# Attention beside a scan: decays in the halves of the context's place in SBUF, turned states in two banks of PSUM

## The reference, cut to what matters

```
x = x + tanh(g_xattn) * ssm(ctx, layernorm(x))
    # state_t = state_{t-1} * exp(delta_t * A[:, n]) + delta_t * u_t * B_t[n]
    # y_t     = sum_n state_t[:, n] * C_t[n]            n = 0..15
x = x + tanh(g_ffn) * layer(layernorm(x))
    # layer: RMS norm, causal attention, output product, RMS norm,
    #        8 routed experts (best 2 per row) and a shared expert
```

## Time and profile before

| What | us |
|---|---|
| median of 3 runs (1787.08 to 1792.86) | 1789.75 |
| the profiled execution | 1790.59 |
| its span, first to last instruction | 1788.8 |
| units of round 0 (attention 0 beside scan 1), 234.6 to 397.2 | 162.6 |
| units of round 1, 481.7 to 645.0 | 163.3 |
| units of round 2, 727.0 to 892.0 | 165.0 |
| DVE busy in the units of round 0 | 149.6 |
| POOL busy in the units of round 0 | 95.9 |

### The profile page before, as it was taken

How to read it: one execution, slowest core, us unless ns; L and a number is a source line. 1 busy time by engine, 2 the same in 40 slices (tenths; PEclk the granted TensorE clock), 3 DMA queues, 4 the chain that set the end, 5 groups by cost and what they waited for, 6 DMA issues and landing times.

```text
span 1788.8 us, 26797 instructions
## 1 busy us (share of the span) xinstructions
PE 1503.7 (84%) x9168; PEld 1150.6 (64%) x9168; DVE 1166.9 (65%) x1699; ACT 916.2 (51%) x2038; POOL 810.2 (45%) x807
## 2 busy tenths in 40 slices
PE   5677967788777789677878998799999999999994
PEld 2344645565445556455655666688787999999973
DVE  5987589996699985899945444432324666566545
ACT  5675457764467753567724663221213666666510
POOL 1992266542466532565413211243422555555444
PEclk8789968899878899788988999899999999999997
DMA  4460001111011111011132004721311877777464
GB/s 168 153 229 19 25 23 55 54 43 54 7 35 55 54 36 31 19 47 54 37 123 95 30 32 160 293 77 59 110 37 65 307 243 253 261 241 253 155 221 165
DMA packets 94664, 195.76 MB, mean 109 GB/s; under 512 B 8945, under 2 KB 25841, under 8 KB 91201
## 3 DMA queue, kind: packets, MB, share of 16 engines
q1 hardware_dynamic: 89408, 177.26, 29.1%
q0 software_dynamic: 5120, 16.78, 2.8%
HBM read 140.40 MB, written 53.61 MB: 108 GB/s over the span
## 4 chain that ended last, share of the span: by engine, by line
PE 55%; DVE 16%; issue 15%; POOL 7%; ACT 5%; DMA 1%; SPq 1%; DVEq 0%; ACTq 0%; POOLq 0%
PE scores L631 21%; PE bank L631 14%; DVE HS L1770 6%; DVE YA L1781 4%; PE bank L705 3%; PE bank L775 3%; POOL GB L2281 2%; PE bank L790 2%; ACT bank L1269 2%; PE bank L825 2%; PE scores L762 2%; POOL yab L2471 2%; PE scores L749 1%; PE bank L1092 1%; PE scores L765 1%
## 5 line engine op out<-in xcount | busy, mean ns | idle before, releaser
L2281 POOL TENSOR_TENSOR GB<-DU,BB 128x512 f32<-128x512 f32 x256 | 326.8, 1298 | 36.1 <-DVE DL L1752 21.2
L1770 DVE TENSOR_TENSOR_SCAN HS<-bank,GB 128x512 f32<-128x512 f32 x224 | 272.0, 1214 | 20.3 <-ACT bank L1269 17.6
L705 PE MATMUL bank<-ident,HS 128*128 128x128 f32 x860 | 165.8, 325 | 120.9 <-DVE YA L1781 104.9
L705 PEld LDWEIGHTS bank<-ident,HS 128*128 128x128 f32 x860 | 115.2, 165 | 166.3 <-DVE YA L1781 129.8
L1269 ACT ACTIVATE bank<-DL,aneg 128x512 f32<-128x512 f32 x224 | 154.7, 691 | 110.0 <-DVE HS L1770 108.2
L775 PE MATMUL bank<-ident,EX 128*128 128x128 f32 x640 | 131.5, 306 | 34.2 <-ACT PT L1314 20.9
L631 PE MATMUL scores<-xth,wgh 128*128 128x256 f32 x552 | 158.1, 286 | 2.2 <-DVE fa L2162 1.3
L1781 DVE SCALAR_TENSOR_TENSOR YA<-bank,Ct,YA 128x512 f32<-128x512 f32 x199 | 147.0, 738 | 14.2 <-PE bank L705 12.8
L631 PE MATMUL scores<-xth,wgl 128*128 128x256 f32 x552 | 156.1, 283 | 0.0
L631 PE MATMUL scores<-xtl,wgh 128*128 128x256 f32 x552 | 156.1, 283 | 0.0
L1314 ACT ACTIVATE PT<-bank 128x128 f32<-128x128 f32 (+3 forms) x256 | 110.3, 431 | 72.0 <-PE bank L775 64.9
(11 more groups left out here) (294 smaller groups left out, 3798.6 us busy)
## 6 DMA issues: line engine op xcount, KB each, us to landing
wgr<-wffn_in SPq DMA_DIRECT2D x108, 384.0 KB, 6.5
wdr<-wffn_in SPq DMA_DIRECT2D x81, 256.0 KB, 3.1
BB<-b_scratch SPq DMA_DIRECT2D x64, 256.0 KB, 3.3
xr<-xg SPq DMA_DIRECT2D x23, 512.0 KB, 5.8
yg<-ysb SPq DMA_DIRECT2D x23, 512.0 KB, 6.5
xg<-V SPq DMA_DIRECT2D x11, 1024.0 KB, 5.8
hah<-hhd SPq DMA_DIRECT2D x5, 1024.0 KB, 14.1
hal<-hhd SPq DMA_DIRECT2D x5, 1024.0 KB, 16.1
```

The source lines that it names most:

```text
L705: mm = nc.tensor.transpose(state_bank(s, q)[:, et * P:(et + 1) * P], HS[:, n % 2, et, tt * P:(tt + 1) * P], ident[:])
L1770: nc.vector.tensor_tensor_scan(HS[:, n % 2, et, :], decay_bank(s, k), GB[:, k % 4, :], 0.0, ALU.mult, ALU.add).then_inc(scan_done, 1)
L2281: nc.gpsimd.tensor_tensor(GB[:, k % 4, :], DU[:, et, :], BB[:, n % 2, :], ALU.mult).then_inc(gb_ready, 1)
```

## The change

Decays of the scans beside attention go by turns into the two halves of `cT` in SBUF instead of the bank HT1, and decay k waits for scan k - 2. HT1 becomes a second bank of turned states: states go by turns into HT0 and HT1, and turn q waits for the addition of state q - 2. The next context can't be loaded into `cT` while decays use it, so its load moves from the start of the round to its end and waits for all 64 blocks of the scan. Nothing else changes.

```diff
             if s == 0:
                 return (HT0, A[0])[q % 2]
-            return (A[0], A[2], A[3])[q - (NB - 3)] if q >= NB - 3 else HT0
+            return (A[0], A[2], A[3])[q - (NB - 3)] if q >= NB - 3 else HT[q % 2]
...
         def z_bank(s, tt):
...
         def decay_bank(s, k):
-            return (HT1, A[1])[k % 2] if s == 0 else HT1
+
+            return cT[:, k % 2, :] if s else (HT1, A[1])[k % 2]
...
         def turned_bank(b, v):
...
             def load_ctx(s):
                 at(sp, xp_mm, T4 * s)
+                if s > 1:
+                    sp.wait_ge(scan_done, NB * s)
                 sp.dma_start(cT[:], ctx_in[s]).then_inc(ctx_in_s, 16)
...
                     sp.wait_ge(xd_ready, s + 1)
                     sp.dma_start(b_scratch[s], xd[DR:DR + NS, :]).then_inc(b_stored, 16)
-                    if 0 < s < B - 1:
-                        load_ctx(s + 1)
                     sp.wait_ge(b_stored, 16 * (s + 1))
                     for n in range(2):
...
                     if b >= 0 and i and m:
                         rows_out(b, i - 1, m - 1)
+                if 0 < s < B - 1:
+                    load_ctx(s + 1)
...
             begin()
...
                     else:
                         pe.wait_ge(kept, 2 * weighed(m, ut) + 2)
-                if s and 0 < q < NB - 3:
-                    pe.wait_ge(y_acc, adds(s, q))
+                if s and 1 < q < NB - 3:
+                    pe.wait_ge(y_acc, adds(s, q - 1))
                 for et in range(T4):
                     mm = nc.tensor.transpose(state_bank(s, q)[:, et * P:(et + 1) * P],
...
                 if n == 0:
                     act.wait_ge(dl_s, T4 * s + et + 1)
-                if k > (s == 0):
-                    act.wait_ge(scan_done, NB * s + k - (s == 0))
+                if k > 1:
+                    act.wait_ge(scan_done, NB * s + k - 1)
                 nc.scalar.activation(decay_bank(s, k), DL[:, et, :], ACT.Exp, scale=aneg[:, et, n:n + 1]
                                      ).then_inc(dA_ready, 1)
```

## The result

The changed kernel takes 1826.18 us (median of 4 runs, 1822.57 to 1828.56) against 1788.90 for the kernel before beside it (4 runs): a ratio of 1.0206, 95% interval [1.0186, 1.0226]. The forecast was 1826, with a range from 1797 to 1860. The profiled run of the changed kernel is the shortest of its four, 1822.57 us with a span of 1820.8; against the earlier trace rows's execution that is 32.0 us more.

A forecast was written before the change was run, and what follows sets the result against it. DVE was taken to set the pace in the three units (busy 149.6 of 162.6 us in the first). Per round 15.0 - 3.6 - 3.0 + 3.8 = 12.2 us, 36.6 in three, gave 1826 against the median; range 1797 to 1860.

The forecast's parts named there:

- the sum: Units of rounds 0 to 2: 15.0 - 3.6 - 3.0 + 3.8 = 12.2 us more per round, 36.6 in three.
- Two places and two banks: DVE's waits in the units: 5.9 us for decays and 3.6 for turned states go, 9.5 per round, 28.5 in three.
- The walk through the quad: One early quad, context to context: scans and POOL products block each other, so 8.56 us becomes 9.3 to 10.4.
- the middle: Early quad: 9.85 us, between 9.3 (scan wins the second gap) and 10.4 (second product first), 1.3 us more.
- The first three intervals: Start of each round's units, `cn` to `cn`: each 1.3 us longer.
- the other twelve: Later intervals of a round: 1.3, 0.8 or 0.75 us more by reduction width, 1.0 for the last, before the corrections.
- The contention: Units: a scan with two SBUF inputs and a POOL instruction reading SBUF each wait for the other, whole.
- The late quads: Last quads of a round: 10.5 to 11.3 us from `cn` to `cn`.
- a criterion for a wrong forecast: Whole kernel: wrong if scans keep 1.21 us beside products, or stretches outside the units move by more than 2 us.
- No contention: Rival, units: the scan does not contend, so only the gain of 9.5 us per round stands, 1761; chance 0.10.
- The well packed queue: Rival, units: a waiting scan always goes before POOL's next instruction, -1.0 us per round, 1787; chance 0.07.
- The lost lead: Rival, units: POOL gets in twice and loses its lead, scans wait for products, 30 us per round, 1880; chance 0.07.

The follow-up runs named there:

- short products: Changed kernel with each POOL product beside attention made for one time step instead of 512: 1757.49 us, ratio 0.9829 to the kernel before.
- the kernel before with the same cut: Kernel before with each POOL product beside attention made for one time step instead of 512: 1778.60 us, ratio 0.9940.
- the place alone: Kernel before with the load moved and decays beside attention in one half of `cT`, old waits, one bank of turned states: 1851.37 us, ratio 1.0349.

## Why the prediction was right

The mechanism was the one forecast: scans with both inputs in SBUF and POOL's reading instructions wait for each other, and that costs more than the waits that go. How well the terms of the sum were sized is less certain.

*What goes.* Two places and two banks were to give 9.5 us per round. With short products on both sides, first scan to last takes 150.8, 149.2 and 149.3 us after and 157.8, 156.7 and 157.4 before, so 7.5 per round, and 21.1 in the whole kernel for a forecast of 28.5. But the scans of the changed kernel still meet `h2l` and `ctl` there: those of a round add up to 79.6 us, for 77.8 in the kernel before with the same cut. If these 1.8 us lie on the path in full, the gain was 9.3 per round, 28 in three, which is an estimate from these rows and about what was forecast.

*What comes.* The walk through the quad was to give gaps of 1.0, 2.25, 1.37 and 1.00 us. Counting 1.21 back from the ends of the scans above, they are 1.01 (from `cn`), 2.16, 1.32 and 0.95. The two ends given for an early quad were 9.3 and 10.4, and the middle was taken. That choice was off: the first three quads of the first round take 10.22, 10.20 and 10.22, since the second product is always there first. The first three intervals grew by 1.45 on average for a forecast of 1.3, the other twelve by 0.66 for 0.69. One by one these twelve lie between -0.85 and 2.24, so the fit of their mean says little for the walk through the later quads. Sums per round, `cn` to `cn`: 12.2, 9.7 and 13.4 for 12.2.

*The terms.* The contention was to cost 36.6 + 28.5 = 65.1 us, and the cut products make it 68.7 less the 9.8 that the cut is worth in the kernel before, 58.9. That is the products' part alone. With the 5.4 us that `h2l` and `ctl` take in the cut kernel, by the estimate above, it is 64. So either both terms were sized about right, or gain and loss were both some 6 to 7 us too large and the errors cancel; no run here cuts `h2l` and `ctl` too, and it stays open. That the sum came within 1 us (37.3 by the medians for 36.6) is luck in part. The units (first scan to last) of the profiled kernel before add up to 480.2 us and those with the load moved alone to 475.8, so like units differ by 4.4 us between two executions; and the sum has no term for the time outside the units, which changed too.

*The signs.* Scans' median over 1.3 (1.59), products up to 2.2 (2.23), hardly a wait of DVE for decays (0.9 us), and units of about 175 us (175.3 to 176.2) are as written. PE's waits for additions were to go, and fell from 30.7 to 12.8 us in the first units. The late quads, forecast at 10.5 to 11.3, spread from 10.1 to 12.7, since finishing work falls into some, and the last interval of all is 8.5. Scans over 1.3 us all start in the midst of a POOL instruction that reads SBUF, though in 13 of 116 cases it isn't a product.

Two more signs were not as written. The in-projection starts 0.7 us sooner behind the last scan, and, a criterion for a wrong forecast, the stretches outside the units moved by more than 2 us: they became 2.4 us shorter, each time. The load isn't the cause (87.3 with the load moved alone, 87.2 with the place alone). The 0.7 goes with the second bank: in the changed kernel with one bank of turned states the in-projection starts 10.0 and 10.7 us behind the last scan. The other 1.6 or so go with TensorE's clock. Here are the 14 us that begin 52 us behind the start of the last scan, in the columns of the units above. The first row is the kernel before, the second the change, the last two the two stretches of the changed kernel with short products, which take 85.5 and 83.8 us:

```profile
446.43:460.43 14.00, 14.00 (x47) 8.44 (x46) 6.25 (x8) 4.76 (x9) 2.94 (x3) 0.88 0.00 0
```

```profile
460.78:474.78 14.00, 14.00 (x51) 8.57 (x51) 6.62 (x9) 4.75 (x8) 2.53 (x2) 1.00 0.00 0
```

```profile
437.07:451.07 14.00, 14.00 (x44) 8.39 (x44) 6.20 (x8) 4.92 (x8) 2.56 (x3) 0.88 0.00 0
671.73:685.73 14.00, 14.00 (x52) 8.56 (x51) 6.88 (x9) 4.95 (x8) 2.52 (x2) 1.00 0.00 0
```

PE is busy throughout in all four. In the kernel before, where PE had been busy without a break from 444.43 on, the granted clock is 1.00 up to 452.43 and 0.51, the lower of its two levels (1.2 GHz for 2.4), from 454.43 to 456.43; its other stretch has the same mean. In both stretches of the changed kernel the clock stays at 1.00, with PE as busy. With short products one program shows both, 1.7 us apart, so it isn't tied to the change alone; why it falls in one stretch and not in another stays open. These are some 3 us of the result for which the prediction had no term. (That the kernel before with short products shows 85.8 has another cause: the shorter instruction for `QK`, which is 1.67 us long again in the changed kernel.) The 2.5 us at the end of the kernel aren't explained; that end is 4.2 us longer with the load moved alone than in the kernel before.

*The rivals.* No contention (1761) fell with the first scan over 1.3 us; the cut kernel at 1757 is what that rival described. The well packed queue (1787) needs the scan to go before the second product, which it didn't in the plain quads. The lost lead (1880) would show DVE waiting for products: 0.2 us in the first units.

## What to carry to other kernels

A buffer moved from PSUM to SBUF may make an instruction of DVE one with two inputs in SBUF; before doing so, look what POOL reads at that time, and price each meeting at what is left of POOL's instruction. Look at an instruction's duration and not at idle time alone: blocked time counts as busy, and a list of waits can get shorter while a kernel gets slower. Where the place is needed, give it to those instructions that run while POOL idles or only writes, and look in the new trace which of them still meet, since the meetings move with the timing.

## What was not expected of the hardware

- A fill by POOL (0.52 to 0.53 us) ran beside scans with two SBUF inputs 83 times without a delay to itself.
- A very short instruction pays most: `rib` went from 0.41 to 1.09 us by the mean. A product of one time step, 0.19 us by the median of the cut kernel, took 1.1 us where a scan was under way.
- The waiting instruction is shown from its issue: a product that waits for a scan takes 2.18 us in the profile, and one without a wait 1.27.
